# Ending a bitonic sort at groups of 128 keys and loading its input in 112 and 13 rows, in a graph network's kernel

## The reference

```python
agg = segment_sum(ln(x)[dst], src, num_segments=6250)    # edge_row = src, edge_col = dst
x = x + ((agg + ln(x)) @ gW1 + gb1) @ gW2 + gb2
y = ln(x)                                                 # layer norm over the 256 numbers
w = softmax(mean(y) @ Wr + br)                            # 8 experts; y goes in as a batch of 1
h = relu(bn1(y @ W1[e] + b1[e]))
h = relu(bn2(h @ W2[e] + b2[e]))
x = x + sum_e w[e] * (h @ Wo[e] + bo[e])
```

## Time and profile before

| | us |
|---|---|
| median of 3 runs | 1456.22 (1455.87 to 1458.68) |
| the profiled execution | 1456.66 |
| its span, first to last instruction | 1454.6 |
| busy in the span: PE / DVE / ACT / POOL | 1230.4 / 1186.9 / 918.4 / 805.1 |

### The profile page before, as it was taken

The page is one execution under the profiler, slowest core; times in us unless marked ns, Lnnn a source line. Parts: engine busy times, 40 slices in busy tenths (PEclk is TensorE's granted clock), DMA queues, the critical chain, the costliest instruction groups (busy, mean ns, idle before and its releaser), DMA issues.

```text
span 1454.6 us, 26399 instructions
## 1 busy us (share of the span) xinstructions
PE 1230.4 (85%) x8370; PEld 823.0 (57%) x8370; DVE 1186.9 (82%) x3444; ACT 918.4 (63%) x1736; POOL 805.1 (55%) x869
## 2 busy tenths in 40 slices
PE   0057675666789888999999999999999999999996
PEld 0035453444566556566666666666666666666665
DVE  6997999776688887888889888897988889787654
ACT  6986855144566555656666576566656666575877
POOL 1200000577777777777777777777777777662000
PEclk9999899768999999999999999999999999999999
DMA  7611022343434343443434334343443434331000
GB/s 233 202 43 45 32 77 69 101 140 107 121 107 124 106 131 106 117 120 106 135 106 135 107 106 136 107 134 106 120 120 106 135 102 132 93 89 55 6 15 16
DMA packets 82189, 150.87 MB, mean 104 GB/s; under 512 B 16808, under 2 KB 54987, under 8 KB 82053
## 3 DMA queue, kind: packets, MB, share of 16 engines
q0 software_dynamic: 39840, 108.84, 26.4%
q1 hardware_dynamic: 42212, 40.36, 8.8%
HBM read 129.87 MB, written 19.27 MB: 103 GB/s over the span
## 4 chain that ended last, share of the span: by engine, by line
PE 59%; DVE 15%; ACT 9%; POOL 6%; issue 5%; DMA 4%; DVEq 1%; ACTq 0%; SPq 0%
PE PA L1424 14%; PE PB L1440 13%; POOL gbuf L486 6%; PE PL L1458 5%; PE PT L1458 5%; PE PN L1458 5%; ACT junk L498 4%; DVE zz L755 3%; DVE zz L756 3%; PE PT L1373 3%; DMA gbuf<-xn_hilo,dsti 3%; DVE acc L1005 2%; PE PN L1352 2%; ACT junk L513 2%; PE PN L1353 2%
## 5 line engine op out<-in xcount | busy, mean ns | idle before, releaser
L486 POOL DMA_INDIRECT gbuf<-xn_hilo,dsti x830 | 788.3, 950 | 371.1 <-issue 226.6
L1424 PE MATMUL PA<-yT,wsplit 128*128 128x512 f16 (+3 forms) x1440 | 293.0, 343 | 2.5 <-DVE h L1089 2.5
L1440 PE MATMUL PB<-h,wsplit 128*128 128x512 f16 (+3 forms) x1440 | 293.4, 342 | 0.0
L664 ACT ACTIVATE h<-PB,bnt,bns 128x512 f16<-128x512 f32 (+3 forms) x240 | 168.0, 700 | 193.7 <-PE PB L1440 192.6
L653 ACT ACTIVATE h<-PA,bnt,bns 128x512 f16<-128x512 f32 (+3 forms) x240 | 167.1, 696 | 160.5 <-PE PA L1424 160.1
L1089 DVE TENSOR_TENSOR h<-PA,h 128x512 f16<-128x512 f32 (+3 forms) x240 | 140.1, 586 | 61.0 <-ACT PA L654 60.3
L1424 PEld LDWEIGHTS PA<-yT,wsplit 128*128 128x128 f16 x1440 | 134.1, 99 | 93.4 <-DVE h L1089 2.8
L1440 PEld LDWEIGHTS PB<-h,wsplit 128*128 128x128 f16 x1440 | 135.4, 99 | 88.9 <-issue 1.9
L1095 DVE TENSOR_TENSOR h<-PB,h 128x512 f16<-128x512 f32 (+3 forms) x240 | 140.1, 587 | 53.9 <-ACT PB L665 53.2
L937 DVE TENSOR_SCALAR onehot<-iota_row,srel 128x128 f16<-128x128 f16 x830 | 180.7, 270 | 0.0
L665 ACT ACTIVATE PB<-PB,bnt,bns 128x512 f32<-128x512 f32 (+3 forms) x240 | 160.2, 668 | 0.0
(11 more groups left out here) (244 smaller groups left out, 1953.1 us busy)
## 6 DMA issues: line engine op xcount, KB each, us to landing
gbuf<-xn_hilo,dsti POOLq DMA_INDIRECT x830, 2.8
xt<-x_whole_bins SPq DMA_DIRECT2D x49, 128.0 KB
out<-xt SPq DMA_DIRECT2D x49, 128.0 KB
acc<-in_x SPq DMA_DIRECT2D x4, 1536.0 KB
x_whole_bins<-acc SPq DMA_DIRECT2D x4, 1536.0 KB, 12.2
xn_hilo<-xt SPq DMA_DIRECT2D x24, 256.0 KB, 2.1
h<-in_L_ffn_W SPq DMA_DIRECT2D x16, 256.0 KB, 3.0
h<-in_L_ffn_Wo SPq DMA_DIRECT2D x8, 256.0 KB, 3.9
```

The costliest lines, as they stand in the source:

```text
L486: pool.indirect_dma_start(gbuf[:, k % SLOTS, :], None, xn_dram, bass.IndirectOffsetOnAxis(dsti[:, k:k + 1], 0)).then_inc(gat[k % SLOTS], 16)
L664: nc.scalar.activation(h2[:, e % 2, 0, h, 0:w], PB[:, h, 0:w], ACT.Relu, bias=sh, scale=sc)
L1424: last = T_.matmul(PA[:, h, 0:w], wsp[0][:, e, k, wp, h * P:(h + 1) * P], yT[:, g % 2, yp, k, 0:w], start=n == 0, stop=n == 5)
L1440: last = T_.matmul(PB[:, h, 0:w], wsp[1][:, e, k, wp, h * P:(h + 1) * P], h1[:, e % 2, yp, k, 0:w], start=n == 0, stop=n == 5)
```

## The change

- **Edges.** Four loads (rows 0 to 111 of the sources and of the destinations, then rows 112 to 124 of both) in place of two of 125 rows. ScalarE makes the float copy of the sources for itself. VectorE makes the keys in two operations; the signs and `dsg` are made before it waits for the edges.
- **Sort.** Half B of j = 7 ends after d = 8, so seven stages are left out, and each tile of 128 sorted keys holds the right keys in some order. The buffer that holds the result changes with the parity.
- **Schedule.** `PmA` is made in one operation of 8 x 18 elements a partition, not in eight of 18, and the first two `Pm` are made after the sort, not between the halves of j = 7.
- **TensorE after the sort.** The eight matmuls of the first entries go in two parts: the even blocks after the last stage's min, the odd ones after its max. Their `warm` starts 4 operations before the end, not 8.
- **Places.** `W_AT` is 6, 3, 3 at (1, B), (2, A), (2, B), in place of 7, 5, 0. `XN_AT` has 2 and 6 at (6, A) and (6, B), in place of 3 and 5. The reciprocal `xrs` moves from before half B of j = 4 to after its stage d = 8.

```diff
+EDGE_ROWS = [(0, 112), (112, 13)]
@@ sync
-            sp.dma_start(edges[0:EP, 0, :], src.rearrange("(p n) -> p n", p=EP)).then_inc(s["edges_in"], 16)
-            sp.dma_start(edges[0:EP, 1, :], dst.rearrange("(p n) -> p n", p=EP)).then_inc(s["edges_in"], 16)
+            for r, n in EDGE_ROWS:
+                sp.dma_start(edges[r:r + n, 0, :], src.rearrange("(p n) -> p n", p=EP)[r:r + n, :]).then_inc(
+                    s["edges_in"], 16)
+                sp.dma_start(edges[r:r + n, 1, :], dst.rearrange("(p n) -> p n", p=EP)[r:r + n, :]).then_inc(
+                    s["edges_in"], 16)
@@ scalar
+            act.wait_ge(s["edges_in"], 32 * len(EDGE_ROWS))
+            nc.scalar.activation(srcf[0:EP, :], edges[0:EP, 0, :], ACT.Copy).then_inc(s["srcf_ready"], 1)
             act.wait_ge(s["srcf_ready"], 1)
             act.wait_ge(s["consts"], 20)
@@ vector
-            dve.wait_ge(s["edges_in"], 32)
+            partition_signs()
+            dve.wait_ge(s["edges_in"], 32 * len(EDGE_ROWS))
             dve.wait_ge(s["keys"], 2)
-            V.tensor_copy(srcf[0:EP, :], edges[0:EP, 0, :]).then_inc(s["srcf_ready"], 1)
-            V.tensor_scalar(keyi[0][0:EP, 0:EF], edges[0:EP, 0, :], BITS, None,
-                            ALU.logical_shift_left).then_inc(s["keys"], 1)
+            V.tensor_scalar(keyi[0][0:EP, 0:EF], edges[0:EP, 0, :], BITS, KEYBASE, ALU.logical_shift_left,
+                            ALU.bitwise_or).then_inc(s["keys"], 1)
...
-            V.tensor_scalar(keyi[0][0:EP, 0:EF], keyi[0][0:EP, 0:EF], KEYBASE, None,
-                            ALU.bitwise_or).then_inc(s["keys"], 1)
@@ schedule, last piece
-                for blk in range(NBLK):
-                    V.tensor_scalar(PmA[:, blk * SLOTS:(blk + 1) * SLOTS], tk[:, 0:SLOTS], pcol[:, blk:blk + 1], None,
-                                    ALU.is_equal).then_inc(s["firsts"], 1)
-                for blk in range(2):
-                    V.tensor_scalar(Pm[blk % 2], tk[:, SLOTS:], pcol[:, blk:blk + 1], None,
-                                    ALU.is_equal).then_inc(s["select"], 1)
+                V.tensor_tensor(PmA.rearrange("p (b n) -> p b n", n=SLOTS),
+                                tk[:, 0:SLOTS].unsqueeze(1).broadcast_to([P, NBLK, SLOTS]),
+                                pcol[:].unsqueeze(2).broadcast_to([P, NBLK, SLOTS]),
+                                ALU.is_equal).then_inc(s["firsts"], 1)
@@ levels across partitions, half B
-                if j == 4:
-                    dve.wait_ge(s["xsd_ready"], 1)
-                    V.reciprocal(xrs[:], xsd[:]).then_inc(s["xrs_ready"], 1)
...
-                for d in range(9, 0, -1):
-                    if d == 1 and j < 7:
+                for d in range(9, 0 if j < 7 else TILE_LOG, -1):
+                    if d == 1:
                         last_step(keyf[cur[0]], keyf[1 - cur[0]], 2)
                     else:
                         halves(keyf[cur[0]], keyf[1 - cur[0]], SW, 1 << d, False)
                     cur[0] = 1 - cur[0]
+                    if j == 4 and d == 8:
+                        dve.wait_ge(s["xsd_ready"], 1)
+                        V.reciprocal(xrs[:], xsd[:]).then_inc(s["xrs_ready"], 1)
...
+            for blk in range(2):
+                V.tensor_scalar(Pm[blk % 2], tk[:, SLOTS:], pcol[:, blk:blk + 1], None,
+                                ALU.is_equal).then_inc(s["select"], 1)
@@ tensor, after the sort
-            pe.wait_ge(s["firsts"], NBLK)
-            warm(pb)
-            pe.wait_ge(s["sorted_step"], next(turn))
-            for blk in range(NBLK):
+            pe.wait_ge(s["firsts"], 1)
+            warm(pb, 6)
+            n = next(turn)
+            for i, blk in enumerate([*range(0, NBLK, 2), *range(1, NBLK, 2)]):
+                if i % (NBLK // 2) == 0:
+                    pe.wait_ge(s["sorted_step"], n - 1 if i == 0 else n)
@@ tables
-W_AT, w_all = shares([(1, "B", 7), (2, "A", 5)])
-XN_AT, xn_all = shares([(4, "B", 4), (5, "A", 3), (5, "B", 5), (6, "A", 3), (6, "B", 5), (7, "A", 4), (7, "B", 1)])
+W_AT, w_all = shares([(1, "B", 6), (2, "A", 3), (2, "B", 3)])
+XN_AT, xn_all = shares([(4, "B", 4), (5, "A", 3), (5, "B", 5), (6, "A", 2), (6, "B", 6), (7, "A", 4), (7, "B", 1)])
+TILE_LOG = 7
-SORTED_IN = (56 + 28 + 70) % 2
+SORTED_IN = (56 + 28 + 70 - TILE_LOG) % 2
```

More of the change, by code:

```diff
@@ L716, in _, with partition_signs @@
             V.memset(keyi[0], PADKEY).then_inc(s["keys"], 1)
-            dve.wait_ge(s["edges_in"], 32)
+            def partition_signs():
+                dve.wait_ge(s["consts"], 2)
+                V.tensor_scalar(gray[:, 0:1], pidx[:], 1, None, ALU.logical_shift_right).then_inc(s["diag"], 1)
+                dve.wait_ge(s["diag"], 1)
+                V.tensor_tensor(gray[:, 1:2], gray[:, 0:1], pidx[:], ALU.bitwise_xor).then_inc(s["diag"], 1)
+                V.tensor_scalar(gray[:, 2:3], pidx[:], 1, None, ALU.bitwise_and).then_inc(s["diag"], 1)
+                dve.wait_ge(s["diag"], 3)
+                for j in range(7):
+                    V.tensor_scalar(gray[:, 3 + j:4 + j], gray[:, 1:2], j, 1, ALU.logical_shift_right,
+                                    ALU.bitwise_and).then_inc(s["diag"], 1)
+                dve.wait_ge(s["diag"], 10)
+                V.tensor_scalar(sgn[:], gray[:, 2:10], -2.0, 1.0, ALU.mult, ALU.add).then_inc(s["diag"], 1)
+                dve.wait_ge(s["diag"], 11)
+                dve.wait_ge(s["consts"], 11)
+                for j in range(7):
+                    V.tensor_scalar(dsg[:, j, :], ident[:], sgn[:, 1 + j:2 + j], None, ALU.mult).then_inc(s["diag"], 1)
+            partition_signs()
+            dve.wait_ge(s["edges_in"], 32 * len(EDGE_ROWS))
             dve.wait_ge(s["keys"], 2)
-            V.tensor_copy(srcf[0:EP, :], edges[0:EP, 0, :]).then_inc(s["srcf_ready"], 1)
-            V.tensor_scalar(keyi[0][0:EP, 0:EF], edges[0:EP, 0, :], BITS, None,
-                            ALU.logical_shift_left).then_inc(s["keys"], 1)
+            V.tensor_scalar(keyi[0][0:EP, 0:EF], edges[0:EP, 0, :], BITS, KEYBASE, ALU.logical_shift_left,
+                            ALU.bitwise_or).then_inc(s["keys"], 1)
             dve.wait_ge(s["keys"], 3)
@@ L866, in _ @@
                 width = -(-EF // m) * m
-                if level == 6:
-                    partition_signs()
                 if level == 10:
@@ L950, in _ @@
                             ALU.logical_shift_right, ALU.bitwise_and).then_inc(s["firsts"], 1)
-            dve.wait_ge(s["firsts"], NBLK + 3)
+            dve.wait_ge(s["firsts"], 4)
             V.tensor_copy(srcs[:, first_columns], srcs[:, first_columns].bitcast(I32)).then_inc(s["firsts"], 1)
-            dve.wait_ge(s["firsts"], NBLK + 4)
+            dve.wait_ge(s["firsts"], 5)
             V.scalar_tensor_tensor(out=srel[:, first_columns], in0=bk[:, first_columns], scalar=-float(P),
@@ L960, in _ @@
                 if blk == 3:
-                    dve.wait_ge(s["firsts"], NBLK + 5)
+                    dve.wait_ge(s["firsts"], 6)
                 if blk >= 3:
@@ L1230, in at, with warm @@
                 return n
-            def warm(bank):
+            def warm(bank, gap=WARM_GAP):
                 n = turn_at[sum(t <= upto[0] for t in turn_at)]
-                if n - upto[0] < WARM_GAP:
+                if n - upto[0] < gap:
                     return
-                pe.wait_ge(s["sorted_step"], at(n - WARM_GAP + 2))
+                pe.wait_ge(s["sorted_step"], at(n - gap + 2))
                 for _ in range(WARM_N):
@@ L1313, in _ @@
                 rows_rest(XN_AT.get((j, "B"), ()))
-            pe.wait_ge(s["firsts"], NBLK)
-            warm(pb)
-            pe.wait_ge(s["sorted_step"], next(turn))
-            for blk in range(NBLK):
+            pe.wait_ge(s["firsts"], 1)
[4 more added lines that the diff above has]
+                    pe.wait_ge(s["sorted_step"], n - 1 if i == 0 else n)
                 last = T_.matmul(PL[:, 1, 0:SLOTS], keyf[SORTED_IN][:, blk * P:(blk + 1) * P],
-                                 PmA[:, blk * SLOTS:(blk + 1) * SLOTS], start=blk == 0, stop=blk == NBLK - 1)
+                                 PmA[:, blk * SLOTS:(blk + 1) * SLOTS], start=i == 0, stop=i == NBLK - 1)
             last.then_inc(s["sched_pe"], 1)
```

20 lines of the change are left out of this document (2 added, 18 removed).

## The result

| | before | after |
|---|---|---|
| median, us | 1456.05 (1455.14 to 1458.68, 4 runs) | 1439.65 (1438.71 to 1440.04, 4 runs) |
| profiled execution / its span | 1456.66 / 1454.6 | 1439.49 / 1437.4 |
| first gather | 263.54 | 244.40 |
| first gather to the end of the span | 1191.06 | 1193.00 |

The ratio is 0.9889 [0.9876, 0.9901]: 16.4 us faster, 1.45 us above the predicted 1438.2. The last two rows hold the whole account. The first gather comes 19.14 us earlier, 1.94 are given back behind it, and 1456.66 - 19.14 + 1.94 = 1439.46.

A forecast was written before the change was run, and what follows sets the result against it. The first gather, waiting for the sort, was taken to hold the whole rest. Leads of 6.0 at (5, A) and 12.1 at (7, B) sum to 18.1 us: 1456.66 to 1438.6 profiled, 1438.2 median, range 1434.5 to 1444.

The forecast's parts named there:

- Edges: Load at the start: the edges land at 6.1 us instead of 12.3, their transfers spread over more engines.
- rival 1: Load at the start: the edges land no earlier, lead about 2.2 at (5, A), time 1442; chance 0.15.
- Signs: Start of VectorE's sort: moved under the load, ending at 5.6 us, they save 2.6 us inside the sort.
- ScalarE's start: Start of counting: table load still ends at 8.33, counting starts at 9.35, not 12.87; lead 3.5 us (2.3 to 5.8).
- rival 2: Start of counting: ScalarE starts at 7.1, its table loaded at the very start; 2.3 us more, 1435.5; chance 0.10.
- (2, A) and (2, B): Both halves of j = 2: fewer weight pieces ahead of the turns on TensorE; leads of 5.0 and 7.7 us.
- (3, A): Half A of j = 3: prep, behind three weight pieces, leads by 3.2 us, the turn's copy by 7.7.
- (5, A): Half A of j = 5: the moved reciprocal ends at 159.6 without waiting for input and sets the turn; lead 6.0 us.
- (5, A) to (7, A): Halves from j = 5 to 7: all moves together, the moved pair fits at (6, B); lead stays 6.0 us.
- (7, B): Half B of j = 7: copy 1.9 earlier, seven stages 9.3, result 0.9 sooner; together 12.1 us (9.8 to 12.4).
- Behind the first gather: From first gather to end: unedited work moves as a block, the same 1191 us; wrong if changed by over 2 us.
- rival 3: From 263.5 to 620 us: TensorE's clock takes back a part, costing 10 us, time 1448; chance 0.07.

The follow-up runs named there:

- the run with the cut alone: Kernel before with only the last sort level shortened (half B of j = 7 ends after d = 8, matmuls in two parts, later warm): 1449.52 us, 0.9957.

## Why the prediction was right

The mechanism was right: the block behind the first gather moved as a whole. That the number came so near is in part luck: terms were missed by 1 to 2 us in both directions, and executions of one program differ by as much. Point by point:

- **First gather.** 18.1 us of lead predicted, 19.1 and 17.3 in two profiles. The profiled execution took 1439.49, 0.9 more than the 1438.6 forecast for it: 1.0 more lead, 1.9 given back behind the first gather.
- **Edges.** 6.78, not 6.1: inside the bounds, at the near end. Undoing the split alone moves the landing to 11.78, so rival 1 is out. Its price was low, though: 1442 forecast for that state, 1444.55 measured. The lead at (5, A) is 2.2 there, as worked out, but the first gather leads by 12.9 and not 14.3: 1.1 is lost at (6, B) and 0.4 in (7, B), and 0.8 more behind it. One reading of the earlier trace rows was loose: the 47 to 71 GB/s fill the first seven slices, 1.9 us; the 2.8 count from the load's issue at 0.74. This is what the Trainium skill, "DMA: Bandwidth & Descriptors", section "Why a DMA increments its semaphore by 16 and not by 1", says of an outer size that 16 divides and one that it doesn't.
- **Signs.** They fitted under the load, but by nothing: 4.0 us from their first row (2.92) to their end, not 2.6. `dsg` took 2.26 where it takes 1.46 inside the sort. With the landing at 6.1 they would have cost 0.8, of a lead that the wait at (2, A) swallows anyway.
- **ScalarE's start** is the mis-sized term. I took the load at its old place, the first pass at 9.35 and a lead of 3.5; rival 2's mechanism held, the table load at 0.73, and the pass came at 7.69: lead 5.2. It was not rival 2's full 5.8, because the edges came 0.7 later. The mechanism that held had a chance of 0.10 in the prediction. I held on to the middle value because its times stood in rows; but the row itself laid the load's wait to a constant that the new first operation doesn't need. The Trainium skill, "ScalarE: Activation LUTs", section "Table sets: the hidden batching unit", has copy in every set, and the trace agrees: one load serves Copy and Sign.
- **(2, A) and (2, B).** Predicted leads 5.0 and 7.7, measured 7.4 and 10.3. 1.7 of the 2.4 is ScalarE's start, the rest the way from the first piece to the copy, 12.5 us and not 13.3. The step between the two points, 2.7, held (2.8). VectorE's own lead held too, 9.7 at (2, A) for the 9.8 predicted; it waits 4.37 there and not 6 to 7 because TensorE came 2.4 earlier.
- **(3, A).** The step from (2, B) was 4.5 down at `prep` (measured 10.3 to 5.8) and back to the same lead (9.8, predicted 7.7). The wait is 2.62; in the second profile 4.30. Part of this lead is no work of the change: the prediction took over from the profile before a turn that ran partly at the lower clock (L1270, 3.78) and a second wait of 0.5. In the run with the cut alone, the same program up to there, the turn took 2.05 and the copy came at 133.98, not 134.97.
- **(5, A).** 6.0 predicted, 7.4 measured against the profile before; the bound was right. In the run with the cut alone this copy comes at 176.97, not 178.34, and against that the lead is 6.0. So the 1.4 are within what executions differ by. The reciprocal didn't wait, as said, and its end at 157.91 (159.6 predicted) set the turn. What came 2.1 early at (3, A) arrived here as 1.4; GpSimd's `xnm` after it took 0.60, not 0.29.
- **(5, A) to (7, A).** The lead stayed 7.37 at both ends, as predicted. The reason given, that a pair moved to (6, B) fits the room there, is neither shown nor refuted: VectorE waits 2.22 at (6, B) before and 2.23 after, each time behind a slow `warm` (4.12 and 3.86 us), which the prediction did not have, and over the profiles this wait varies by 2 us with either tables. That the two were equal is luck.
- **(7, B).** 12.1 predicted, 11.8 measured: 2.0 to the copy (1.9), 9.3 for seven stages (9.3), 0.5 and not 0.9 for the hand-over, since `warm` lasts until 241.16, the end of the sort, and leaves the even blocks no start ahead of it.
- **Behind the first gather.** Predicted unchanged within 2 us; 1.94 more. Counted from the first gather, the 500th and 1000th of TensorE's matmuls after it (at 112 and 186 us) come when they did before within 0.4, the 2500th (at 420) comes 1.4 later, and from there to the end it stays at 1.3 to 1.9. That is where the stretch that gathers pace turns into the one that TensorE fills. Is it the change? The run with the signs inside the sort has the same program behind the first gather and a distance of 1191.03; the seven profiles of the kernel after and its other variants in these batches have 1191.8 to 1193.3. So this distance moves by 2 us between executions of what is there one program, and I can't say that any of the 1.9 belongs to the change. The rows give rival 3, TensorE's clock, no support: its mean from the first gather to 620 us is 0.93, before it was 0.92.

## What to carry to other kernels

Ask at each meeting of two engines who comes last, and count only that engine's lead: the signs' 2 us on VectorE were worth nothing, edges that land 5 us earlier at both engines 4.9. An engine that warms up in front of a waiting partner should not: drop the warm-up where its engine comes straight from other work (three of them brought 5.6 us here); where it came from idling, at (6, B) and behind the sort, leaving it out changed nothing that the medians show. When two parts of a change meet in one idle time, as the short last half and the single `PmA` do, price them together. And take a second profile before reading a difference of 1 or 2 us out of one: the first gather of one program moved by 1.8.

## What the runs showed of the hardware

- The activation table (1.28 us) is loaded somewhere among the waits of the first operation that uses it. Where Sign came first, waiting for the copy and for the constants, the load stood behind the constants (7.05 and 7.55), in the first case 5 us ahead of the copy; where Copy came first, waiting for the edges alone, it stood ahead of that wait (0.73). What decides between two waits was not varied.
- TensorE's clock after short idling: `warm` took 2.47 us behind 1.39 of idling, 2.50 behind 1.74, 4.12 and 4.13 behind 2.67 and 2.66, 4.12 behind 3.30, 4.03 and 4.61 behind 3.39, and 3.86 behind 4.45. But it took 4.63 behind 1.71 in the run with 125 rows, where the work ahead of the idling already ran at the lower clock. The same `L1217` took 3.72 in one execution and 5.41 in another behind the same 1.11 of idling, so the idle time ahead doesn't settle it alone.
- Small operations on VectorE were slower at the start, while GpSimd made its constants and the edges were loading: seven of 128x128 took 2.26 us, 1.46 inside the sort; one of 128x8 0.69, against 0.17. Which of the two slowed them was not varied.
- The same kernel took 1642.9 us in one batch, on another chip, with nearly the same lengths of single operations up to the first gather. From then on engines wait longer for each other, and TensorE's mean granted clock is lower (0.82 against 0.92 from there to 620 us, 0.98 against 1.00 behind that); which of the two causes the other is open.
